# A mixture-of-experts layer in blocks of 128 rows: one more block is transposed by DMA, and ScalarE loads two registers earlier

## The reference

```
x = x + layernorm(x) @ (weight * elem_mask).T          # 2048 tokens, 1024 features
h = layernorm(x)
logits = h @ W_gate + b_gate                           # 8 experts
_, top_idx = top_k(logits, 2)
y_all = relu(einsum('bsd,edh->bseh', h, W_e) + b_e)
x = x + take_along_axis(y_all, top_idx[..., None], axis=2).mean(axis=2)
```

## Time and profile before

| what | value |
|---|---|
| time, median of 3 | 645.83 us (645.32 to 657.08) |
| time of the profiled execution | 645.89 us |
| its span in the trace | 644.2 us |
| TensorE busy | 626.6 us |
| VectorE, ScalarE, GpSimd busy | 371.0, 355.3, 276.0 us |

### The profile page before, as it was taken

How to read it: one execution, slowest core, us unless ns; L and a number is a source line. 1 busy time by engine, 2 the same in 40 slices (tenths; PEclk the granted TensorE clock), 3 DMA queues, 4 the chain that set the end, 5 groups by cost and what they waited for, 6 DMA issues and landing times.

```text
span 644.2 us, 11278 instructions
## 1 busy us (share of the span) xinstructions
PE 626.6 (97%) x3495; PEld 508.0 (79%) x3498; DVE 371.0 (58%) x647; ACT 355.3 (55%) x434; POOL 276.0 (43%) x252
## 2 busy tenths in 40 slices
PE   7999999999999999999999999999999999999994
PEld 5666777788788878878888888888888878788873
DVE  5896597887977683454346146035333343499851
ACT  7767764766775633525444443544446346465572
POOL 2013212223655246554555354445535356374623
PEclk9999999999999999999999999999999999999995
DMA  8992874589865357989989779757989999965640
GB/s 349 407 406 81 331 289 164 194 333 330 289 246 211 141 170 226 255 189 228 252 221 236 184 195 226 176 168 216 261 210 217 253 209 257 218 101 99 99 70 2
DMA packets 89207, 140.25 MB, mean 218 GB/s; under 512 B 58304, under 2 KB 58304, under 8 KB 89152
## 3 DMA queue, kind: packets, MB, share of 16 engines
q1 hardware_dynamic: 25776, 92.85, 40.1%
q0 software_dynamic: 11376, 33.57, 23.5%
q10 hardware_dynamic: 52000, 13.11, 12.6%
HBM read 87.59 MB, written 46.14 MB: 208 GB/s over the span
## 4 chain that ended last, share of the span: by engine, by line
PE 87%; ACTq 5%; ACT 3%; issue 1%; DMA 1%; DVE 1%; SPq 0%; POOLq 0%
PE psO L577 76%; ACTq L1215 4%; PE psT L869 2%; PE psT L610 2%; PE psT L577 2%; PE psO L610 1%; PE psG L683 1%; ACT x2T L1224 1%; DMA xb<-data_t 1%; ACT xb L1264 1%; PE psS L664 1%; PE psT L651 0%; PE psO L953 0%; PE psT L953 0%; ACT rows_b L1224 0%
## 5 line engine op out<-in xcount | busy, mean ns | idle before, releaser
L577 PE MATMUL psO<-slots,xT 128*128 (+1 forms) x1728 | 397.8, 391 | 1.3 <-ACT psO L1168 0.8
L577 PEld LDWEIGHTS psO<-slots,xT 128*128 128x128 f32 x1728 | 322.9, 188 | 69.3 <-issue 3.2
L1589 DVE CAST slots<-raw 128x1024 fp32r<-128x1024 f32 x56 | 57.6, 1029 | 186.5 <-DMA raw<-L_ffn_W_e 105.0
L577 PE MATMUL psO<-wT,xT 128*128 128x512 f32 x624 | 152.3, 397 | 0.0
L577 PEld LDWEIGHTS psO<-wT,xT 128*128 128x128 f32 x624 | 114.3, 188 | 25.1 <-issue 2.7
L1264 ACT ACTIVATE xb<-psO 128x512 f32<-128x512 f32 x72 | 43.0, 597 | 159.7 <-PE psO L577 117.5
L2016 POOL DMA_INDIRECT rows_out<-xb,tok_of x33 | 62.2, 1884 | 152.1 <-ACT xb L1264 124.3
L2010 POOL TENSOR_TENSOR xT<-x2T,xT 128x1024 fp32r<-128x1024 f32 x35 | 88.8, 2538 | 22.4 <-ACT xT L1232 11.8
L1591 DVE TENSOR_TENSOR slots<-raw,slots 128x1024 fp32r<-128x1024 f32 x56 | 68.7, 1227 | 1.9
L1168 ACT ACTIVATE psO<-bias_slot 128x512 f32 (+1 forms) x72 | 43.4, 602 | 41.0 <-issue 23.0
L1936 POOL TENSOR_SCALAR rs<-squares 128x1 f32<-128x1 f32 x16 | 8.7, 545 | 70.5 <-ACT rows_a L1017 40.9
(11 more groups left out here) (297 smaller groups left out, 640.4 us busy)
## 6 DMA issues: line engine op xcount, KB each, us to landing
raw<-L_ffn_W_e SPq DMA_DIRECT2D x56, 512.0 KB
x_rows<-x SPq DMA_DIRECT2D x16, 512.0 KB, 4.5
xb<-data_t SPq DMA_DIRECT2D x12, 512.0 KB, 4.1
mask_stage<-mask_blocks SPq DMA_DIRECT2D x8, 512.0 KB, 10.6
w_stage<-weight_t SPq DMA_DIRECT2D x8, 512.0 KB, 11.4
row_stage<-L_attn_weight SPq DMA_DIRECT2D x8, 512.0 KB, 12.5
xr<-L_attn_data SPq DMA_DIRECT2D x8, 512.0 KB, 5.8
x_planes<-planes_even SPq DMA_DIRECT2D x8, 512.0 KB, 3.0
```

Of the source, the lines that this page charges most:

```text
L577: last = eng.matmul(psum, xT[:, p, a, kt, :], moving(b, kt), start=(i == 0 and kt == 0 and not seeded), stop=(i == len(PASSES) - 1 and kt ...
L1589: eng.tensor_copy(slots[:, e % 2, HI, kt, :], raw[:, kt % 2, :]).then_inc(c_split, 1)
```

## The change

Block 3 is now a block that goes by DMA. The constant in VectorE's table for SyncE and the assertion follow from it. GpSimd's gather of block 3, now from x2_planes, stands behind the clearing of x2[:, 1, :]. Since block 3 takes no turn on TensorE, the later blocks' rows change places among the tiles rows_a, rows_b and x2, and turned_odd and turned_even swap. Apart from that, ScalarE's two register loads for block b + 1 stand ahead of the relu of block b's first half, from block 3 on; for block 2 they stay behind it.

```diff
         def by_dma(b):
-            return b > EARLY + 2 and (b % 2 == 1 or b >= TAIL)
+            return b > EARLY and (b % 2 == 1 or b >= TAIL)
...
             for b in range(EARLY, SURE):
-                if b > EARLY and not by_dma(b + 1):
+                if not by_dma(b + 1):
                     transpose_rows(b + 1)
...
-                    if b == EARLY and n == 0:
-                        transpose_rows(b + 1)
...
-            def biases_of(b):
-
-                if b < EARLY:
-                    return None
-                if b == EARLY:
-                    eng.wait_ge(c_tab_d, 15)
+            def slot_and_ready(b):
                 slot = eng.value_load(slot_of[0:1, b - EARLY:b - EARLY + 1], min_val=0, max_val=1)
                 ready = eng.value_load(ready_of[0:1, b - EARLY:b - EARLY + 1], min_val=2 * KT, max_val=2 * KT * N_EXP)
-                eng.wait_ge(c_split, ready)
-                return slot
+                return slot, ready
...
                 if b >= 2:
                     eng.wait_ge(l_add[b % 2], 16 * (b // 2))
+                slot = None
+                if b + 1 > EARLY:
+                    slot, ready = slot_and_ready(b + 1)
                 for n in range(NH):
                     relu(b, n)
-                    if n == 0:
-                        slot = biases_of(b + 1)
+                    if n == 0 and b + 1 == EARLY:
+                        eng.wait_ge(c_tab_d, 15)
+                        slot, ready = slot_and_ready(b + 1)
+                    if n == 0 and b + 1 >= EARLY:
+                        eng.wait_ge(c_split, ready)
                     seed_half(b + 1, slot, n)
                     if n == 0 and b + 3 < N_BLOCKS and by_dma(b + 3):
                         turn_rows(b + 3)
...
             gather_rows(2)
-            gather_rows(3)
             eng.wait_ge(c_planes, NB)
             eng.memset(x2[:, 1, :], 0.0).then_inc(c_clear, 1)
+            gather_rows(3)
             add_rows(0)
```

More of the change, by code:

```diff
@@ L406, in build @@
         assert TAIL % 2 == 0 and not by_dma(TAIL - 2)
-        assert [b for b in range(TAIL) if by_dma(b)] == list(range(5, 5 + 2 * N_TURNS, 2))
+        assert [b for b in range(TAIL) if by_dma(b)] == list(range(3, 3 + 2 * N_TURNS, 2))
         def turn_bank(b):
@@ L1825, in _ @@
             eng.wait_ge(c_pace, KT)
-            eng.tensor_scalar(turn_part[:], turn_no[:], -3.0, None, ALU.add).then_inc(c_pace, 1)
+            eng.tensor_scalar(turn_part[:], turn_no[:], 1.0, None, ALU.add).then_inc(c_pace, 1)
             eng.tensor_scalar(tail_part[:], turn_no[:], float(5 - 2 * TAIL), 0.0, ALU.add, ALU.max).then_inc(c_pace, 1)
```

## The result

| | mean of the runs compared | ratio to the kernel before, 95% interval |
|---|---|---|
| changed kernel | 664.0 us (663.07 and 664.98) | 1.027 [1.0197, 1.0343] |
| kernel before, same chip | 646.5 us (645.32, 645.83 and 648.49; the median of all four of its runs is 647.16) | |

The forecast was 654.8 us with a range up to 661.5. The sign was right, and the size was short by some 9 us. Executions that the chip disturbed as a whole are in no ratio here, but five profiles are of such executions: those of the changed kernel (673.30 us, span 671.6), of the loads alone and of the three controls. The changed kernel's late part is therefore shown a second time further down, from the trace of nearly the same kernel.

The account below looks back on a forecast made before the run. TensorE, busy 626.6 us of the 644.2 us span, was taken as the bound. From 645.89 us, + 8.4 (stall) + 2.2 (clock) - 0.87 (transposes) - 0.8 (loads) = + 8.9 gave 654.8 us; 80% range 651.5 to 661.5.

Parts of the forecast that it names:

- Part 3: ScalarE in block 0: the transpose waits for gather 3, delaying relu and seed; TensorE stalls 8.4 us, bounds 7.5 and 17.5.
- Part 1: TensorE in block 2: the eight transpose matmuls of block 3 go, a gain of 0.87 us.
- part 2: ScalarE in block 2: a join replaces copies for block 3, 1.5 us more work, hidden in idle time.
- Rival C: Not slower: the DMA queue takes the wait, not ScalarE; 644.2 us, chance 0.06 with anything else on the fast side.
- part 4: TensorE behind the stall: its clock falls and costs 2.2 us, from nothing to 3.5.
- part 5: Loads ahead of the relu gain 0.8 us from 498 on; other edits unchanged; block 5's slow issue could make its seed 2.5 us late.
- The gain of the loads: ScalarE from 498 on: shorter gaps ahead of seeds cut TensorE's waits by 0.8 us, bounds 0 and 1.3.
- part 3's silent half: TensorE behind the stall: later work shifts with it, and none of the 8.4 us is won back.
- The prediction's own warning: It is wrong if TensorE has no gap at 236, one over 13 us, or later gaps adding more than 2 us.
- rival A: A much longer stall in block 0: gather 3 takes 8.4 us, the issue 4 to 5.4; 661 us, chance 0.20.

Follow-up runs that it names:

- the loads alone: The kernel before with only the register loads moved ahead of the relu of a block's first half; ratio 0.9996.
- the three controls: The kernel before with four more DMA transposes nobody reads, the fourth moved twice; ratios 1.0149, none (649.08 us in one run), and 1.0063.
- the stall alone: The kernel before with one wait added on ScalarE in block 0, for the landing of block 3's gather; ratio 1.0119, 7.7 us.
- block 3 alone: The changed kernel with the register loads left behind the relu, so only block 3 going by DMA is new; ratio 1.028.

## Why the prediction was right, and where it failed

**Right: the stall and its mechanism.** Part 3 had the stall at 8.4 us from 236.2, ended at 244.6; it was 7.55 us, ended at 243.92. The transpose was forecast for 241.7 and stood at 241.15, 4.4 us behind its gather, near the bound of 4.3 and not the 5.2 taken; the issue was forecast at 1.46 and took 1.44. The chain from the table of tokens over memset, gather, issue, relu and seed holds link by link, and the stall alone cost 7.7 us of time with its clock. Part 1 (0.87 us) and part 2 (join hidden) are as forecast. Rival C is out: the wait did hold ScalarE.

**The clock: the fall right, its size by luck.** The clock fell to 0.50 and cost 2.0 us (1.5 to 2.5 in the profiles of the stall alone and the other kernels with block 3's issue in block 0), and 2.2 were forecast. But part 4 took the size from the start of the program, and the view of stretches of the kernel before gives the full clock there:

```profile
3.00:6.50 3.50, 3.50 (x35) 3.46 (x36) 0.85 (x5) 1.94 (x4) 2.40 (x16) 1.00 0.99 383
```

So the slower matmuls of rows 12 don't show a low clock, and no row of before had the size. The rule of the Trainium skill (TensorE: Matmul & The Clock Gate, "What's actually happening") that idleness brings the lower level back agrees with 0.50 in 244 to 248.

**Sizes that were off, small.** Block 5's issue took 3.63 us and not 1.46, and the second stall of 1.64 us that part 5 kept in the range came. The shorter stall and this second one nearly cancel: 9.6 us at block 23, against 9.7. The gain of the loads, 0.8 us, is too small for the interval of their run.

**The step that failed** is in part 5: "the other ring tile for the rows of later blocks, turned_even and turned_odd swapped, a constant in the table of SyncE's waits. Each has the same count and size as before." That is true of the tiles, as two runs showed, and it passed over the thing that did change: the position of every later transpose in ScalarE's sequence of transposes. With it fell part 3's silent half: nothing is given back, and nothing more was thought to be taken. The late part costs 6.4 us in the trace with block 3 alone (5.0 to 6.7 in four of the kernels with one issue added, 13.1 in the fifth), nearly as much again as the stall, and the sum had nothing for it. The prediction's own warning named it ("if later gaps add more than 2 us") without a case for it; rival A came near the time, with 661 us, by a longer stall, which didn't happen.

**Shown and not shown.** Shown by ratios: neither the loads, the stall, the two turned tiles nor the row tile makes the late loss, and one further transpose costs 0.8%. Shown by traces, one of each kernel: with one further transpose the late gaps are there, with four they aren't; no ratio alone separates these two. Nor is a mere shift in time the cause, since the stall alone shifts the late part by 7.8 us and the controls by 14.8 to 27.7 (at block 23's transpose), with 0.5 to 2.0 us of late loss. Argued only: the way from the place to the gap, as the gaps differ in place between executions and one goes another way. Open: why every fourth issue is short, and why the loads of the weights took so long in two of the profiles.

None of the versions beats the kernel before.

## What to carry to other kernels

A DMA added early in an instruction stream may change the issue times of all later ones of its kind. List the durations of such issues by their running number, and check which block gets the cheap one where the pipeline has no slack. An issue that waits for data should stand where the engine has nothing behind it that TensorE wants: here 15 us of waiting ahead of a 0.60 us seed cost 7.55 us and the clock, while the work removed was worth 0.87.

## What the hardware showed that I had not expected

- The issue of a DMA_TRANSPOSE of 128x2048 elements of 16 bits out of SBUF holds ScalarE's stream for 1.33 to 15.17 us. The Trainium skill (DMA: Bandwidth & Descriptors, "Issuing engines are not separate DMA queues") calls such time usually small beside the DMA. The traces don't agree: block 27's issue took 6.84 and 7.26 us where the way from its end to the landing took 7.3 and 9.9.
- Every fourth issue is short, whatever the tiles: median 1.43 us against 3.15 to 3.46. Four of the 103 took more than 2.4 us: 2.60, 2.71, 8.40 and 12.12.
- The last two of these, and the longest of all, 15.17 us, were issues that began 0.04 to 3.9 us behind the end of another. Not all of those are slow (seven others took 1.8 to 4.2 us); with 4 us or more between, the longest was 8.61 us.
- Behind the stop of 7.55 us TensorE's clock stood at its lower level from 244 to 248 and was full from 248 on.
